# Moving three DRAM-to-DRAM copies of x and one ScalarE copy in a recurrent, routed layer

## The reference

```
h_t = h_{t-1} * A + xn_t              # per channel, along each sequence
s   = h @ BC                          # [8192, 512] @ [512, 512]
e   = argmax(xn @ gate_w.T)           # one of 8 experts for each token
out = x + s * silu(xn + xn @ expert_w[e].T)
```

## Time and profile before

| | |
|---|---|
| Median of 3 runs | 516.46 us (516.45 to 517.62) |
| The profiled execution | 516.83 us, of which the span of the core is 515.1 us |
| PE busy | 495.1 us, 96% of the span |
| DVE, POOL, ACT busy | 410.1 us, 322.4 us, 260.1 us |
| Granted TensorE clock, mean | 0.991 of full speed |
| First phase | from 0 to about 255 us of the span |
| Moved by DMAs | 114.27 MB, 39.1% of the 16 engines' span by q1 (SP), 31.7% by q0 (GpSimd) |

### The profile page before, as it was taken

One profiled execution on the slowest core, in us unless ns is written; L12 is line 12 of the kernel. 1 busy time (PEld: TensorE's weight loads), 2 busy tenths in 40 slices (PEclk: granted clock), 3 DMA queues, 4 the chain that ended last, 5 costly groups with the idle time before them and its releaser, 6 DMA issues. The chain is left out here.

```text
span 515.1 us, 10723 instructions
## 1 busy us (share of the span) xinstructions
PE 495.1 (96%) x2739; PEld 388.5 (75%) x2740; DVE 410.1 (80%) x1075; ACT 260.1 (50%) x500; POOL 322.4 (63%) x362
## 2 busy tenths in 40 slices
PE   7999999999999999999988999999999999999993
PEld 6667777777777777777766888888788888887882
DVE  5999899989899989898844777777777777776773
ACT  4676776786687677677422333333333333333330
POOL 2567666666766766766663766656666666646652
PEclk9999999999999999999998999999999999999997
DMA  7978788887877877876245577777777776766620
GB/s 235 350 264 263 222 258 248 246 243 234 271 226 244 271 208 259 257 228 213 104 113 203 185 244 241 237 234 243 234 229 231 230 239 215 231 208 206 216 83 9
DMA packets 65538, 114.27 MB, mean 222 GB/s; under 512 B 9994, under 2 KB 28042, under 8 KB 65504
## 3 DMA queue, kind: packets, MB, share of 16 engines
q1 hardware_dynamic: 47328, 62.46, 39.1%
q0 software_dynamic: 18176, 51.47, 31.7%
HBM read 65.96 MB, written 55.08 MB: 235 GB/s over the span
## 5 line engine op out<-in xcount | busy, mean ns | idle before, releaser
L1073 PE MATMUL ps_s<-w_hi,split 128*128 x284 | 118.3, 417 | 0.1
L643 ACT ACTIVATE ps_s<-ps_s 128x512 f32<-128x512 f32 x71 | 41.3, 582 | 151.5 <-PE ps_s L1075 151.5
L509 POOL DMA_INDIRECT out_dram<-work x71 | 73.2, 1032 | 68.9 <-DVE work L890 59.0
L1074 PE MATMUL ps_s<-w_lo,split 128*128 x284 | 112.6, 396 | 0.0
L1075 PE MATMUL ps_s<-w_hi,split 128*128 x284 | 112.4, 396 | 0.0
L418 POOL TENSOR_TENSOR split<-work,split 128x1024 fp32r<-128x1024 f32 x32 | 77.5, 2421 | 48.6 <-ACT split L571 48.5
L977 PE MATMUL ps_s<-bc_hi,split 128*128 128x512 f32 x256 | 104.1, 407 | 0.7 <-DVE bc_lo L790 0.6
L978 PE MATMUL ps_s<-bc_lo,split 128*128 128x512 f32 x256 | 101.3, 396 | 0.0
L499 POOL DMA_INDIRECT work<-token_rows,work x67 | 69.6, 1038 | 21.7 <-issue 19.8
L436 POOL DMA_INDIRECT slot_table<-token_id,slot_id x64 | 63.0, 984 | 31.6 <-issue 21.1
L685 DVE TENSOR_TENSOR_SCAN work<-a_col,work,ps_xt 128x256 f32<-128x256 f32 x112 | 74.2, 721 | 0.0
(11 more groups left out here) (118 smaller groups left out, 737.9 us busy)
## 6 DMA issues: line engine op xcount, KB each, us to landing
token_rows<-work SPq DMA_DIRECT2D x31, 528.0 KB, 3.2
work<-in_L_attn_inputs_dram SPq DMA_DIRECT2D x31, 512.0 KB, 4.7
token_rows<-work SPq DMA_DIRECT2D x29, 512.0 KB, 5.5
work<-in_L_ffn_expert_w_dram SPq DMA_DIRECT2D x128, 64.0 KB, 4.2
slot_table<-w_lo SPq DMA_DIRECT2D x1, 2080.0 KB, 12.8
token_rows<-in_L_attn_inputs_dram SPq DMA_DIRECT2D x3, 512.0 KB, 10.6
out_dram<-work POOLq DMA_INDIRECT x71, 3.3
work<-token_rows,work POOLq DMA_INDIRECT x67, 4.4
```

Of the source, the lines that this page charges most:

```text
L509: nc.gpsimd.indirect_dma_start(out=out_flat, out_offset=bass.IndirectOffsetOnAxis(ap=slot_tok[:, n:n + 1], axis=0), in_=o_sb[:, u], in_off ...
L1073: nc.tensor.matmul(z_ps[v], hi, wh, start=(k == 0), stop=False)
L1074: nc.tensor.matmul(z_ps[v], hi, wl, start=False, stop=False)
```

## The change

SP no longer issues the three copies ahead of its loop. The first four rounds are written out, and `copy_x(c)` stands behind `store_s(c)` in rounds 0 to 2. On ScalarE, in groups 1 to 3, `copy_parts(c + 1)` stands ahead of both halves of `normalise` instead of between them.

```diff
             sp.wait_ge(empty_ready, 1)
             nc.sync.dma_start(table_fill, ...).then_inc(table_empty, 16)
-            for c in range(XR - 1):
-                copy_x(0, c)
             sp.wait_ge(pad_ready, 1)
-            with sp.Fori(0, GROUPS // 4 - 1) as it:
+
+            def round_of(it, c):
+                next_x(it, c)
+                store_x(it, c + XR - 1)
+                load_w(it, c + WR)
+                store_s(it, c)
+
+            for c in range(4):
+                round_of(0, c)
+                if c < XR - 1:
+                    copy_x(0, c)
+            with sp.Fori(1, GROUPS // 4 - 1) as it:
                 for c in range(4):
-                    next_x(it, c)
-                    store_x(it, c + XR - 1)
-                    load_w(it, c + WR)
-                    store_s(it, c)
+                    round_of(it, c)
...
                 if left >= 1:
                     high_part(it, c + 1)
+                early = not start and c < 4
+                if early:
+                    copy_parts(it, c + 1)
                 if left >= 2:
                     normalise(it, c + 2, 0)
-                if left >= 1 and not start:
+                if left >= 1 and not start and not early:
                     copy_parts(it, c + 1)
                 if left >= 2:
                     normalise(it, c + 2, 1)
```

## The result

| | before | after |
|---|---|---|
| Median of 16 runs each, us | 516.16 | 518.26 |
| Lowest to highest, us | 514.41 to 517.62 | 516.46 to 519.63 |
| The profiled execution and its span, us | 516.83, 515.1 | 517.80, 516.1 |

The changed kernel is slower: the ratio is 1.0036, with a 95% interval of 1.0022 to 1.005, which is 1.1 to 2.6 us. (Before's median over these 16 runs stands beside the 516.46 of the three runs shown at first.)

A forecast was written before the change was run, and what follows sets the result against it. TensorE was taken as the bound. Waits behind the copies left ScalarE 2.4 us behind, TensorE 2.05 after 0.35 in hand; 516.83 + 2.05 = 518.9, less 0.37 for the median gave 518.5 us, 8-in-10 range 515.9 to 520.0.

The forecast's parts named there:

- TensorE is the bound and keeps a delay: Groups 4 to 31: TensorE busy for 205.48 of 205.58 us, so a delay ahead of it reaches the end.
- ScalarE's part is worth -0.3 us: Group 1: scores copied ahead of both normalise halves gain 0.3 to 0.4 us at TensorE; groups 2 and 3 cost 0.
- The copies delay stores 4 to 6: SP's queue, rounds 0 to 2: each copy adds 1.5 us ahead of the stores; ScalarE waits 0.2, 1.1 and 1.4 us.
- The wait for store 6: Third copy: store 6 lands at 55.0 against a need at 53.6, so ScalarE waits 1.4 us.
- the backlog of the second round: SP's queue after the second copy: round 1's store of s is 1.1 us behind, carried on to store 6.
- the slack of 0.1 to 0.2 us that I gave store 6: Kernel before: store 6 lands at 52.4 to 52.5, normalise needs it at 52.58.
- The total: Whole kernel: 516.83 + 2.05 = 518.9 us profiled; 518.5 us as the median of the runs.
- The rival that the queue takes the copies in: SP's DMA queue: a copy costs under about 0.6 us net; 516.1 to 516.9 us, chance 0.33.
- The rival of a dear copy: Rounds 0 to 2: a copy costs more than 2.5 us; 521 to 523 us, chance 0.05.
- The rival that TensorE's whole pause goes: TensorE at the scores: the full 1.14 us pause is gained and stays; 515.3 us, chance 0.07.

The follow-up runs named there:

- the kernel with the copies alone: Changed kernel with ScalarE's old order, so only the three copies are moved; groups 2 to 8 in 46.56 us, total 1.0045 against before.
- The doubled copies: Changed kernel with a second same-size copy, into a buffer nothing reads, behind each of the three; groups 2 to 8 in 48.55 us, total 1.0095 against before.
- one copy: Changed kernel with only group 0's copy behind the store of s, the others at the start; groups 2 to 8 in 45.25 us, total 1.0007 against before.

## Why the prediction held

- **TensorE is the bound and keeps a delay.** Right, and more exactly than I could expect: from group 8 to 31 all kernels but the one with copies in rounds 12 to 14 take 174.85 to 175.10 us, whatever was lost ahead of it.
- **ScalarE's part is worth -0.3 us.** Right. The pause at the scores shrank by 0.95 us, and TensorE's transposes of group 3 then waited for their halves, so that the product behind them began at 31.90 instead of 32.25 us. Alone it gave 0.3 us from group 2 to 8, in two profiles. With the copies the gain was gone by group 4, as forecast: the product behind its transposes began at 39.80 us, before at 39.84.
- **The copies delay stores 4 to 6.** Right in kind: the same stores, ScalarE as the engine that waits, TensorE waiting for ScalarE. Store 4 landed at 37.8 (forecast 37.6) and store 5 at 46.8 (46.3), and ScalarE's waits were 0.2 and 1.4 us where I had 0.2 and 1.1. The wait for store 5 hit its number in part by luck. ScalarE was ready at 45.48 us, fifteen of the store's sixteen parts had landed by 45.78, and only the last came at 46.84; in the second profile it was ready at 46.32, with parts fifteen and sixteen at 46.40 and 47.39. So about 1.0 us of each wait is one late part, which my steps did not have. Without one, in the kernel with the copies alone, the same 1.4 us over the kernel before arose at stores 4 and 6.
- **The wait for store 6** is the step that failed, as a size. I let the backlog of the second round (1.1 us) and the third copy (1.5) add up on store 6, for a wait of 1.4. It landed at 53.9 instead of 55.0, 1.5 us over before, and ScalarE did not wait. TensorE, for which I had pauses of about 2 us at groups 5 and 6 together, paused at group 5 alone, by 1.04 us. My sum for the first phase was 2.05 us, and it came to 1.5. Two things went into the missing 1.1 us. The delay was smaller: the fifteenth part of store 6 landed at 53.57 us, 2.1 after the 51.45 of before, where I had 2.6. And the landing I started from was itself late: before, the last part came 1.0 us behind the fifteenth (52.46), in the changed kernel 0.3. So the slack of 0.1 to 0.2 us that I gave store 6 hung on one late part; in the repeat with ScalarE's part alone, where no part was late, it landed 1.4 us ahead of normalise (51.94 and 53.32). The doubled copies show that delays add up to less than I took: there I expected the full 1.3 to 1.5 us for each further copy, and got 0.6 to 0.7. What absorbs the backlog may be the longer round and the stretches in which the DMA engines had been waiting; neither was measured by itself.
- **The total.** 518.5 forecast, 518.26 measured. Part of this nearness is luck: the first phase had 0.5 us less than I added, and I added it to 516.46, where the kernel before came to 516.16 over all its runs. The first phase gives 1.5 us in one profile and about 1.4 in the other (221.8 and 221.6 against 220.2), and the measured difference of the medians was 2.1; its interval, 1.1 to 2.6 us, holds both. The 0.6 us by which the medians differ beyond the first phase's 1.5 us is within that interval and not explained.
- **The rival that the queue takes the copies in** holds for their place ahead of s and falls for the one that the change chose. The pause of the DMA engines ahead of the store of s is real room, but a copy issued behind that store does not reach it before the load and the store of x have been held up. **The rival of a dear copy** fell: store 4 landed 1.6 us later than before (37.78 against 36.14), and with one copy ScalarE's wait for it was 0.26 us, as for a copy of about 1.5 us. Dearer is what rounds 12 to 14 showed, with 2.2 us for the first copy, but not over 2.5. **The rival that TensorE's whole pause goes** fell at the transposes of group 3.

No version here beats the kernel before by what can be measured. The best by their first phase have ScalarE's new order and the copies at the start, in the last rounds or, in the repeat, ahead of s. They save 0.2 to 0.4 us there and come out at 0.9993 to 1.0021 in total.

## What to carry to other kernels

A transfer that nobody waits for can still have a price: it is paid by whoever waits for what stands behind it in the queue. So look for the next DMA in the queue whose landing an engine waits for, read its slack, and put the free transfer behind that DMA and ahead of the pause, which is here one place earlier in the same round. Read a slack from more than one profile: the slack of 0.1 us on which the largest wait of the forecast rested was 1.4 us in another profile. Add up delays round by round only with care: here three further copies cost 0.6 to 0.7 us each, about half of the 1.33 us that a copy takes in a full queue. And measure a fraction of a microsecond as a duration between two marks of the bound engine in the profile; totals that wander by 3 us needed many runs to show 1.5.

## What the runs showed that was not expected

- The last of a DMA's sixteen parts can land about a microsecond behind the other fifteen, and in the changed kernel's two profiles this decided the wait for store 5. In the first profile with the copies ahead of s it was 2.7 us on the store of s, and the wait behind it cost TensorE 1.9 us and then 3.4 us at 0.51 of its clock. Over all fourteen profiles, 922 DMAs that SP issued between 28 and 246 us have all sixteen times (the loads of w left out), and in 45 of them the last came over 0.65 us behind the fifteenth. They mostly come with 16 KB instruction packets, which stand among the DMA packets of the core, take 0.9 to 1.4 us each, and appear three times in this stretch of each profile. Of the 105 DMAs that landed within 9 us of the start of such a packet 35 were late in this way, of the other 817 only 10. In the kernel before the first packet ran at 44.2 us: store 5 (44.13 and 44.49) had nearly landed, and load 7 and store 6 were late by 1.0 us. In the changed kernel it ran at 44.3 us, when store 5, itself delayed, was still on its way. That would fit a packet that holds up one of the sixteen parts. But no run moved the packets, and the 2.7 us are longer than one packet takes; the cause is not shown.
- The second phase wanders more than the whole change is worth: from the transposes of group 31 to the end it took 269.9 to 273.3 us over these profiles. The five profiles in which the first phase ran without waits for copies and with ScalarE's new order have 270.8 to 273.3 us; the kernels that had lost time to the copies have 269.9 to 270.7. That could be a gain given back later, and could be why the 0.3 us never shows in a total. But before (270.5) and the kernel with one copy (270.2) don't fit well, and nothing was tried on it.
